# Convolution, softplus and rings of a state-space layer rearranged, its sum over the states as ordinary fp32 products

## The reference, cut to what matters

```
xz = LN(h) @ in_proj_w.T;  x, z = split(xz)            # 512 channels each
x  = silu(causal_conv(x, 4 taps) + conv_b)
dt, Bm, C = split(x @ x_proj_w.T, [16, 16, 16])        # rank 16, 16 states
dt = softplus(dt @ dt_proj_w.T + dt_proj_b)
h_t = exp(dt_t * A) * h_(t-1) + dt_t * B_t * x_t       # per channel and state
y_t = sum over the 16 states of h_t * C_t
out = (y + x * D) * silu(z) @ out_proj_w.T
```

## Time and profile before

| | |
|---|---|
| median of three runs | 2207.96 us |
| the profiled execution | 2209.55 us, span 2207.8 us |
| mean granted TensorE clock | 0.842 of 2.4 GHz |
| busy over the span | PE 72%, PEld 60%, DVE 53%, ACT 42%, POOL 42% |
| state-space stage | 0 to 660 us; scans from 58.8 to 644.8 us |
| landing of one CB load | 4.7 us |

### The profile page before, as it was taken

How to read it: one execution, slowest core, us unless ns; L and a number is a source line. 1 busy time by engine, 2 the same in 40 slices (tenths; PEclk the granted TensorE clock), 3 DMA queues, 4 the chain that set the end, 5 groups by cost and what they waited for, 6 DMA issues and landing times. The chain is left out here.

```text
span 2207.8 us, 28322 instructions
## 1 busy us (share of the span) xinstructions
PE 1581.1 (72%) x9844; PEld 1326.5 (60%) x9844; DVE 1167.8 (53%) x2195; ACT 919.3 (42%) x1615; POOL 923.0 (42%) x585
## 2 busy tenths in 40 slices
PE   4784884875877973881127997897783099989990
PEld 2654654654764873880015986795683088878880
DVE  5865965965766971225566435645856023322322
ACT  4775675675864441542106222744331023222320
POOL 3655655656663324653005111603005732685406
PEclk7887987987998995995557998799896599999995
DMA  3000100100003023421010001002005221333003
GB/s 128 20 20 19 39 20 20 39 26 33 20 1 89 1 82 113 153 105 39 1 46 1 1 1 42 1 1 78 1 1 207 88 77 49 124 103 117 30 20 117
DMA packets 51960, 114.46 MB, mean 52 GB/s; under 512 B 13996, under 2 KB 34377, under 8 KB 44276
## 3 DMA queue, kind: packets, MB, share of 16 engines
q1 hardware_dynamic: 43764, 75.23, 9.8%
q0 software_dynamic: 8064, 37.45, 5.1%
HBM read 87.02 MB, written 25.87 MB: 51 GB/s over the span
## 5 line engine op out<-in xcount | busy, mean ns | idle before, releaser
L813 POOL TENSOR_TENSOR HC<-H,CB 128x1024 f32<-128x1024 f32 x128 | 307.6, 2404 | 172.8 <-DVE H L724 86.4
L413 PE MATMUL ps<-ident,UT 128*128 128x128 f32 x1024 | 187.8, 314 | 102.5 <-DVE H L724 96.5
L413 PEld LDWEIGHTS ps<-ident,UT 128*128 128x128 f32 x1024 | 138.1, 161 | 186.0 <-DVE H L724 96.6
L567 ACT ACTIVATE UT<-DTXT,BT 128x512 f32<-128x512 f32 x256 | 181.7, 711 | 73.1 <-PE ps L413 73.0
L724 DVE TENSOR_TENSOR_SCAN H<-dA,ps 128x512 f32<-128x512 f32 x128 | 154.6, 1214 | 80.8 <-ACT dA L577 42.9
L724 DVE TENSOR_TENSOR_SCAN H<-dA,HL,ps 128x512 f32<-128x512 f32 x128 | 160.7, 1275 | 49.9 <-PE ps L413 25.7
L577 ACT ACTIVATE dA<-DT,nA 128x512 f32<-128x512 f32 x256 | 181.1, 709 | 0.1
L424 PE MATMUL ps<-ident,HC 128*128 128x128 f32 x1024 | 174.8, 302 | 3.6 <-POOL HC L813 2.2
L1730 POOL TENSOR_TENSOR f_W<-f_stage,f_zeros 128x2048 fp32r<-128x2048 f32 x24 | 86.5, 3606 | 146.2 <-POOLq L1750 138.5
L424 PEld LDWEIGHTS ps<-ident,HC 128*128 128x128 f32 x1024 | 140.4, 159 | 4.8 <-POOL HC L813 2.7
L1947 DVE TENSOR_TENSOR f_XN<-f_XN,ps 128x1024 f32<-128x1024 f32 x39 | 47.7, 1222 | 173.3 <-PE ps L147 173.3
(11 more groups left out here) (480 smaller groups left out, 4348.0 us busy)
## 6 DMA issues: line engine op xcount, KB each, us to landing
f_stage<-in_f_w POOLq DMA_DIRECT2D x24, 1024.0 KB, 5.5
CB<-m_c_rows SPq DMA_DIRECT2D x16, 1024.0 KB, 4.7
f_w<-in_f_w SPq DMA_DIRECT2D x16, 1024.0 KB
f_rows_in<-f_zeros SPq DMA_DIRECT2D x13, 384.0 KB, 13.9
f_DI<-f_rows_in SPq DMA_DIRECT2D x39, 128.0 KB, 2.2
f_rows_out<-f_EO SPq DMA_DIRECT2D x39, 128.0 KB, 1.7
a_values<-a_zeros SPq DMA_DIRECT2D x8, 320.0 KB, 5.5
a_VBD<-a_values SPq DMA_DIRECT2D x8, 320.0 KB, 4.4
```

The lines of the kernel that those rows point to most:

```text
L413: ins = pe.transpose(PS[4 + G % UR][:, t * P:(t + 1) * P], UT[:, n % 2, t, c * P:(c + 1) * P], g.ident[:, :])
L567: act.activation(UT[:, N % 2, t, :], DTXT[:, k % 2, t, :], ACT.Copy, scale=BT[:, k % 2, t, n:n + 1]).then_inc(ut_ready, 1)
L813: pool.tensor_tensor(HC[:, y:y + 2, :], H[:, s:s + 2, :], CB[:, n // 4 % CR, n % 4:n % 4 + 1, :].to_broadcast([P, 2, W]), ALU.mult).then_i ...
```

## The change

- Convolution: VectorE reads x from the PSUM bank, without a copy to SBUF: the full tap first, then three shifted ones on columns j to 511. The three missing columns' part that comes from the chunk before is computed on GpSimd in five small operations (`edges`, p=2, odd chunks) from saved columns (`tail`) and added by VectorE (`add_edge`, p=19).
- Softplus: for chunks 1 to 3 GpSimd does (1+e)-1 in two tensor_scalar and e minus that (`correct`, p 30 to 36), and both sums (`add_logarithm`, p 42 to 54), then dt*x (p 44 to 56). VectorE keeps only the maximum. For chunk 0 VectorE does all of it (`correct_first`, `finish_first`).
- Rings: six dA buffers in place of four, two CB buffers in place of three, own buffers for EA and GD. The first six decays stand ahead of the first chunk's loop.
- Order: the pieces stand at other p (below).
- Sum over the states: `is_transpose=True` is gone from `sum_up`.

```diff
-UR, HR, YR, AR, CR = 2, 8, 8, 4, 3
+UR, HR, YR, AR, CR = 2, 8, 8, 6, 2
@@ sum_up
-                                        start=(u == 0), stop=(u == NU - 1), is_transpose=True, skip_group_check=True)
+                                        start=(u == 0), stop=(u == NU - 1), skip_group_check=True)
@@ TensorE loop
-                            if 2 <= p < 10:
+                            if p in (2, 3, 4, 5):
                                 project_x(k + 1, (p - 2) // 2, p % 2)
-                            if 31 <= p < 35:
-                                project_rows(k + 1, p - 31)
+                            if p in (10, 11, 14, 15):
+                                project_x(k + 1, 2 + (p - 10) // 4, p % 2)
+                        if k and p in (8, 9, 12, 13):
+                            transpose_gated(k - 1, (8, 9, 12, 13).index(p))
+                        if p in (12, 13, 18, 19):
+                            add_skip(k, (12, 13, 18, 19).index(p))
+                        if p in (16, 17, 20, 21):
+                            project_z(k, (p - 16) // 4, p % 2)
+                        if k + 1 < NK:
+                            if 23 <= p < 27:
+                                project_rows(k + 1, p - 23)
+                            if p == 27:
                                 transpose_b(k + 1)
-                            if 36 <= p < 40:
-                                project_dt(k + 1, p - 36)
-                            if p in (52, 54, 56, 58):
-                                transpose_dtx(k + 1, (p - 52) // 2)
+                            if 28 <= p < 32:
+                                project_dt(k + 1, p - 28)
+                        if k and 32 <= p < 40:
+                            project_out(k - 1, (p - 32) // 2, p % 2)
+                        if k + 1 < NK and p in (46, 50, 54, 58):
+                            transpose_dtx(k + 1, (p - 46) // 4)
@@ ScalarE loop: silu at p 20 (was 29), keep_rows 27, keep_b 28, magnitude 29 to 32
+                            if p == 40:
+                                for c in range(CI):
+                                    logarithm(k + 1, c)
+                        if k + 1 < NK and p in (47, 51, 55, 59):
+                            keep_dtx(k + 1, (p - 47) // 4)
@@ silu_x
+                    if k % KB:
+                        act.wait_ge(edge_added, k // KB + 1)
@@ convolve
+                    o, x = DT[:, k % 2, c, :], PS[6 + c % 2]
+                    w = conv_w[:, c, DC - 1 - j:DC - j]
+                        ch.add(dve.tensor_scalar(o, x[:, :], w, conv_b[:, c:c + 1], ALU.mult, ALU.add))
+                    ins = dve.scalar_tensor_tensor(o[:, j:W], x[:, 0:W - j], w, o[:, j:W], ALU.mult, ALU.add)
@@ GpSimd, correct and add_logarithm
+                    pool.wait_ge(exp_ready, k * CI + c + 1)
+                    sums(pool.tensor_scalar(DTX[:, c, :], EA[:, c, :], 1.0, 1.0, ALU.mult, ALU.add))
+                    sums(pool.tensor_scalar(DTX[:, c, :], DTX[:, c, :], 1.0, -1.0, ALU.mult, ALU.add))
+                    pool.tensor_tensor(DTX[:, c, :], EA[:, c, :], DTX[:, c, :], ALU.subtract).then_inc(corr_ready, 1)
...
+                    sums(pool.tensor_tensor(DTX[:, c, :], DTX[:, c, :], EA[:, c, :], ALU.add))
+                    pool.tensor_tensor(o, o, DTX[:, c, :], ALU.add).then_inc(dt_ready, 1)
```

More of the change, by code:

```diff
@@ L241, in mamba @@
         XN = sb("m_XN", [P, TC, D])
-        XC = sb("XC", [P, CI, DC - 1 + W])
+        EA = sb("EA", [P, CI, W])
+        tail, edge = sb("conv_tail", [P, CI, DC - 1]), sb("conv_edge", [P, CI, DC - 1])
+        edge_part = sb("conv_edge_part", [P, CI, DC - 1])
         XS = sb("XS", [P, CI, W])
@@ L582, in _ @@
                     keep_columns(0, j)
-                for c in range(CI):
-                    keep_x(0, c)
                 act.wait_ge(var_ready, 2)
@@ L598, in _ @@
                     logarithm(0, c)
+                act.wait_ge(na_ready, 2)
+                for G in range(AR):
+                    decay(G)
                 for c in range(CI):
@@ L608, in _ @@
                             times_b(k * NS + p // CI + 1, p % CI)
[L609 to L617, removed]
+                        if k or p >= AR:
+                            decay(k * NU + p)
+                        if k + 1 < NK and 1 <= p < 3:
+                            keep_columns(k + 1, p - 1)
+                        if k and p in (9, 10, 13, 14):
+                            keep_gated(k - 1, (9, 10, 13, 14).index(p))
+                        if p == 20:
                             if k + 1 < NK:
@@ L632, in _ @@
                                 silu_z(k, t)
-                        if k + 1 < NK:
-                            if p == 48:
-                                for c in range(CI):
-                                    logarithm(k + 1, c)
-                            if p in (53, 55, 57, 59):
-                                keep_dtx(k + 1, (p - 53) // 2)
-                for t in range(TC):
-                    keep_gated(NK - 1, t)
+                        if k + 1 < NK and p in (47, 51, 55, 59):
+                            keep_dtx(k + 1, (p - 47) // 4)
+                for i in range(TC):
+                    keep_gated(NK - 1, i)
             @block.vector
             def _(dve):
-                ch = Chain(dve, conv_step)
+                ch, fix = Chain(dve, conv_step), Chain(dve, corr_step)
                 def statistics(lo, hi):
@@ L666, in convolve @@
                 def convolve(k, c, j):
[L668 removed]
+                    o, x = DT[:, k % 2, c, :], PS[6 + c % 2]
+                    w = conv_w[:, c, DC - 1 - j:DC - j]
                     if j == 0:
[L670 to L673 removed]
+                        dve.wait_ge(in_full, k * CI + c + 1)
+                        ch.add(dve.tensor_scalar(o, x[:, :], w, conv_b[:, c:c + 1], ALU.mult, ALU.add))
                         return
                     ch.sync()
[L676 removed]
+                    if j == DC - 1 and k % KB == 0:
+                        dve.tensor_copy(tail[:, c, :], x[:, W - DC + 1:W])
+                    ins = dve.scalar_tensor_tensor(o[:, j:W], x[:, 0:W - j], w, o[:, j:W], ALU.mult, ALU.add)
                     if j < DC - 1:
@@ L679, in convolve, with add_edge @@
                     else:
-                        ins.then_inc(conv_ready, 1)
+                        ins.then_inc(conv_done, 1)
+                def add_edge(k):
+                    dve.wait_ge(edge_ready, k // KB + 1)
+                    dve.wait_ge(conv_done, (k + 1) * CI)
+                    o = DT[:, k % 2, :, 0:DC - 1]
+                    dve.tensor_tensor(o, o, edge[:, :, :], ALU.add).then_inc(edge_added, 1)
                 def rectify(k, c):
@@ L789, in add_corrected, with edges @@
-                def add_corrected(k, c):
+                ch, sums = Chain(pool, edge_step), Chain(pool, sum_step)
+                def edges(k):
+                    pool.wait_ge(conv_done, k * CI)
+                    w = lambda j, n: conv_w[:, :, j:j + 1].to_broadcast([P, CI, n])
+                    ch(pool.tensor_tensor(edge[:, :, :], tail[:, :, :], w(0, 3), ALU.mult))
+                    ch(pool.tensor_tensor(edge_part[:, :, 0:2], tail[:, :, 1:3], w(1, 2), ALU.mult))
+                    ch(pool.tensor_tensor(edge[:, :, 0:2], edge[:, :, 0:2], edge_part[:, :, 0:2], ALU.add))
+                    ch(pool.tensor_tensor(edge_part[:, :, 2:3], tail[:, :, 2:3], w(2, 1), ALU.mult))
+                    pool.tensor_tensor(edge[:, :, 0:1], edge[:, :, 0:1], edge_part[:, :, 2:3], ALU.add).then_inc(edge_ready, 1)
@@ L821, in _ @@
                 ins.then_inc(diag_ready, 1)
-                head(1)
-                for c in range(CI):
-                    correct(0, c)
-                for c in range(CI):
-                    add_corrected(0, c)
-                for c in range(CI):
-                    times_x(0, c)
                 for k in range(NK):
```

140 lines of the change are left out of this document (61 added, 79 removed).

## The result

The changed kernel takes 2227.15 us, the median of four runs (2223.89 to 2227.26), against 2207.19: ratio 1.0084, 95% interval 1.0066 to 1.0101. (The ratio is taken over all runs; the two medians alone stand 20.0 apart, 0.90%.) Forecast were 2198.5 and faster. The profiled execution took 2227.19 (span 2225.4), so the sum is to be held against +17.6, not -9.4.

The account below looks back on a forecast made before the run. It took the state-space stage as bound by VectorE in the convolution and a GpSimd-TensorE-scan ring from p=44, then largely by TensorE. Terms summed to -9.4 from 2209.55: 2200, or 2198.5 as median; own range 2185 to 2212, whole range 2165 to 2232.

Parts of the forecast that it names:

- start: Before the first scan: VectorE takes over GpSimd's three passes, six early decays, no copy of x; together -3.5 us.
- p 8 to 24: Steps 8 to 24 of a chunk's 64: TensorE becomes the bound, silu stops it; +2.4, +1.2, +1.2, last chunk +7.
- p 24 to 32: Steps 24 to 32 of a chunk: TensorE 16.9 plus 1.4; +0.4 three times, last chunk -5.4.
- p 32 to 44: Steps 32 to 44 of a chunk: GpSimd the bound, logarithm block stops the scan; -1.7 three times, last chunk +9.5.
- p 44 to 64: Steps 44 to 64 of a chunk: the ring comes once in four steps, not two; -11, -11 and -10.
- clock: TensorE's clock can fall in the 11 stops; 10 us at the lower level, half lost: +5, between 0 and +40.
- the edge addition: VectorE's addition at p=19, ahead of the scan of p=20 and the silu block: 0.2 us, under the slack.
- the round: From p=44, four steps of GpSimd's work plus the way round through TensorE and scan: 11.1 to 11.9, taken 11.6.
- A: Rival, slower: stops leave TensorE, now the bound, at the lower clock for longer; 37 lost, 2231; chance 0.27.
- B: Rival, much faster: the ring opens, a round costs GpSimd's 8.3, stops at p=40 and 44 go; 2153; chance 0.12.
- C: Rival, no change: GpSimd's tensor_scalar costs as a two-input pass, 1.18; 12 us longer, 2210; chance 0.12.
- D: Rival: transposes do not hold the clock up, products do; all stretches at 2.4 GHz; -10, 2189; chance 0.10.

Follow-up runs that it names:

- experiment 5: Changed kernel with four more unused fp32 products of 512 columns on TensorE at p=22 of each chunk: 2219.11 us.
- experiment 1: Changed kernel with the sum over the states as transposes again: 2183.48 us, ratio 0.9893 to the kernel before.
- experiment 10: Changed kernel with project_rows as products of full width, 128 columns in place of 48: one run, 2212.2 us, with other numbers in the layers behind.
- experiment 9: Changed kernel, products kept, with three dt*x transposes two steps later and ScalarE's three blocks three steps later: 2156.86 us, ratio 0.9773 to the kernel before.
- experiment 8: Changed kernel with transposes for the sum, three dt*x transposes two steps later and ScalarE's blocks three steps later: 2123.46 us, ratio 0.9625 to the kernel before.
- experiment 6: Changed kernel with four dA buffers in place of six: 2224.81 us, ratio 1.008 to the kernel before.
- experiment 4: Changed kernel with the first three dt*x transposes and their copies two steps later: 2193.59 us, ratio 0.9942 to the kernel before.
- experiment 2: Kernel before with only the sum made of ordinary fp32 products: 2222.21 us, ratio 1.0074 to the kernel before.

## Why the prediction was wrong

Most mechanisms were those that I named; the sizes of three terms were off, and as the sum was a small difference of large ones, its sign with them. One wait that I had put at nothing was not nothing, and one bound was named wrongly. By the terms of the sum, in us, chunks 0 to 2 and the last together:

| term | predicted | measured |
|---|---|---|
| start | -3.5 | -1.8 |
| p 0 to 8 | +8.0 | +8.4 |
| p 8 to 24 | +11.9 | +26.9 |
| p 24 to 32 | -4.2 | +0.3 |
| p 32 to 44 | +4.4 | +4.4 |
| p 44 to 64 | -32.5 | -22.0 |
| tail and the rest of the program | +1.5 | +1.4 |
| clock | +5.0 | within the rows above |
| sum | -9.4 | +17.6 |

- **The step of p 8 to 24** failed most, by 15: "the silu block now lies at p=20 and stops it for 3.2", and the clock as one line of +5. TensorE's pace was right (2.22 a step where I had 2.17 to 2.2). Three things were not. First, its idle time: 5.10, 3.48, 5.12 and 3.48 in the four chunks, where I had 3.2 three times and 2, which makes 5.6. By the trace the excess in chunks 0 and 2 is the edge addition, which I had put at 0.2 and "under the slack" and which takes 1.84 and 1.85; in the last chunk it is the product of z at p=21. Second, what stands behind the stop: the lower clock costs 5.6 to 8 over four chunks (experiment 5), where I had put +5 for all eleven stops. That I booked the clock as one small line, not with each stop, was the error. Third, the last chunk: the stretch grew by 12.3 where I had 7.1; with transposes again (experiment 1) it is 29.9 in place of 39.1.
- **p 44 to 64**: the round has the parts that I gave it. Of the range 11.1 to 11.9 I took the middle; the way round was at the lower clock each time (3.64), and a round 12.1. Three rounds in three chunks, 4.5 of the 10.5. The rest is the entry, where from the scan of p=44 to that of p=47 11.6 pass in chunks 1 and 2 in place of 10.2 (u and the sum at the lower clock again), and the last five steps of chunk 2, 8.8 in place of 6.5.
- **p 24 to 32**: narrow products and their neighbours cost 2.47 to 2.53 a step in place of 2.17 (experiment 10). The trace of before had this, u at 0.49, the sum at 0.53 and the product of 48 columns at 0.99 from start to start:

```profile
130.32 0.66 PE L413 MATMUL ps<-ident,UT 128*128 128x128 f32 x4
130.81 0.60 PE L424 MATMUL ps<-ident,HC 128*128 128x128 f32 x4
131.34 1.06 PE L353 MATMUL ps<-XS,w_x 128*48 128x512 f32 x2
132.33 0.66 PE L413 MATMUL ps<-ident,UT 128*128 128x128 f32 x4
```

I read 0.44 from another stretch and used it for all.

- **p 32 to 44**: the size came out, the bound only in chunk 0. There the scan stops for 9.4 at p=40, behind GpSimd's fourth correction. In chunks 1 and 2 the scans of p 32 to 40 stand 2.2 apart, TensorE's pace, and TensorE is busy for 26.57 of 27.30, GpSimd for 23.36. With the blocks moved the stretch takes 27.0 with products (experiment 9) and 23.5 to 23.8 with transposes (experiment 8).
- **Start**: dt\*x ended at 48.64, where I had 48.7, though not by my numbers: 39 and twelve passes of 0.68 make 47.2; the corrections ended at 40.1. But six decays in ScalarE's queue ahead of the copies held these back, so +1.7. I had called them a gain; with four of them the first scan is 1.3 earlier (experiment 6).
- **The sum's products**: 0.89 per four against 0.87 taken, 256 times, is 5 of TensorE's time over the stage, inside the rows above. The rule of four times (the Trainium skill, TensorE: Matmul & The Clock Gate, Terms) is refuted at this shape by the row itself: 0.90 for the sum's products and 0.44 for transposes.
- **Right**: VectorE's relief (p 8 to 24 lost its VectorE bound), GpSimd's tensor_scalar (0.62 and 0.1 of wait, 0.70 and 0.1 taken), nothing from the dA ring, and the last chunk as the place of the loss, though 18 in place of 11.7.
- **Rivals.** The time fell where A put it (2231), and A's mechanism is shown for one place, at 5.6 to 8 of the 37 that it asked for. That the number came close is partly luck: A is not the whole cause, and the mean clock rose from 0.85 to 0.91. B did not happen, and experiment 4 shows what it takes. C is excluded by the row of 0.62. D had half of the truth: transposes alone held full clock, yet products hold it through stretches in which transposes let it fall (experiment 2: 1.00 for 0.82). The rule of the Trainium skill that D rests on (TensorE: Matmul & The Clock Gate, PE-mode transpose), that full clock does not engage for transposes, is too strong for these traces: ten us of them ran at 1.00.

What stays open is the rest of the 15 of p 8 to 24: 5.6 is TensorE's idle time, read from the trace, and 5.6 to 7.1 the clock behind it, by experiment. For the 2 to 4 that are left the trace points at the last chunk's p=8 and 9, where TensorE comes from the idle steps of p 5 to 7 at the lower clock (the scans stand 3.7 and 2.7 apart, before 1.5 and 2.1). This was not tried, nor was a kernel without the edge addition, or with z's second product ahead of the block.

## What to carry to other kernels

Where a change makes another engine the bound, price every stop anew at that engine: here TensorE brought u in 0.90 behind a stop in place of 0.44, and that was free only while it had slack. An order written by hand should put a block of another engine's queue where that engine has most work done ahead; here three steps later were worth 35 us and two more buffers nothing. A small operation that such a block waits for needs a price of its own: the edge addition, forecast at 0.2, took 1.85. And before a queue blocks on a result, let it do what the next result depends on: two steps' shift of a transpose was worth 34.

## What the runs showed of the hardware

- An fp32 product of 128x128 takes 0.22 at full clock, a transpose of the same size 0.11.
- A product of 48 output columns by 512 takes 0.99 in the stream, one of 128 columns 0.86; the transposes and products beside it also slow down, 0.49 for 0.44 and 0.99 for 0.89, at a granted clock of 1.00.
- Work whose results nobody uses, put into an idle stretch of TensorE, made the kernel 8.0 faster in the medians; 5.6 of it are behind the filled stops of chunks 0 to 2.
- VectorE's scalar_tensor_tensor with one input in PSUM takes 0.73 beside GpSimd; with both in SBUF it took 1.15 in the mean.
- VectorE's edge addition, 12 elements a partition with both inputs in SBUF, took 1.84 to 1.87 in all 20 places (two in each kernel that has it). Each time it started 0.53 or 0.54 behind a product of GpSimd of 2.3 to 2.4 and ended 0.02 to 0.04 after it.
